# Cross-attention on one core: the value products of a unit in two halves of 8 tiles

## The reference

```python
q = _split_heads(hidden_states @ w_q, HEADS)
k = _split_heads(text @ w_k, HEADS)
v = _split_heads(text @ w_v, HEADS)
out_text = _merge_heads(_sdpa(q, k, v))
k_ip = _split_heads(ip_h @ w_k_ip, HEADS)
v_ip = _split_heads(ip_h @ w_v_ip, HEADS)
out_ip = _merge_heads(_sdpa(q, k_ip, v_ip, mask=mask_ip))   # mask from boxes on a 64 x 32 grid
out = (out_text + IP_SCALE * out_ip) @ w_out + b_out + residual
```

## Time and profile before

| | us |
|---|---|
| median of 3 runs | 456.08 (455.82 to 456.23) |
| profiled execution, its own time | 456.7 |
| its span, first to last instruction | 454.9 |
| TensorE busy | 431.4 |
| VectorE busy | 351.6 |
| ScalarE, GpSimd busy | 133.1, 157.0 |

### The profile page before, as it was taken

How to read it: one execution, slowest core, us unless ns; L and a number is a source line. 1 busy time by engine, 2 the same in 40 slices (tenths; PEclk the granted TensorE clock), 3 DMA queues, 4 the chain that set the end, 5 groups by cost and what they waited for, 6 DMA issues and landing times.

```text
span 454.9 us, 14459 instructions
## 1 busy us (share of the span) xinstructions
PE 431.4 (95%) x6594; PEld 336.6 (74%) x6594; DVE 351.6 (77%) x466; ACT 133.1 (29%) x190; POOL 157.0 (35%) x129
## 2 busy tenths in 40 slices
PE   2877999989999999999999999999999999999997
PEld 2856678867777777777777777777777777777775
DVE  0722578989888888889978898888888988888712
ACT  2402265535222432232233322243223322222200
POOL 1500255845522542336222652254233622232200
PEclk9969799999999999999999999999999999999999
DMA  8998022230213311142113221331124211112333
GB/s 315 340 399 316 1 62 87 71 96 3 63 55 122 115 48 49 48 159 93 54 49 117 96 71 55 128 101 49 48 66 158 82 49 48 49 49 71 101 135 115
DMA packets 23726, 46.97 MB, mean 103 GB/s; under 512 B 2673, under 2 KB 2801, under 8 KB 23665
## 3 DMA queue, kind: packets, MB, share of 16 engines
q1 hardware_dynamic: 23664, 46.05, 29.8%
HBM read 35.55 MB, written 10.49 MB: 101 GB/s over the span
## 4 chain that ended last, share of the span: by engine, by line
PE 92%; DVE 3%; DMA 2%; issue 1%; SPq 1%; ACT 1%
PE ps L557 65%; PE ps L598 12%; PE ps L582 10%; PE ps L641 2%; DMA eye_sb<-in_eye 2%; PE ps L631 1%; PE ps L670 1%; DVE x_lo L507 1%; DVE prob_t L489 1%; DVE prob_t L490 1%; SPq L233 1%; PE ps L646 0%; DVE prob_t L487 0%; DVE text_max L420 0%; DVE prob L426 0%
## 5 line engine op out<-in xcount | busy, mean ns | idle before, releaser
L307 POOL TENSOR_TENSOR prob<-prob,rden 128x1104 f32<-128x1104 f32 x40 | 82.4, 2059 | 262.2 <-DVE rden L449 262.2
L557 PE MATMUL ps<-x_hi,wq_hi 128*128 128x512 f32 x200 | 84.6, 423 | 4.0 <-DVE x_lo L507 4.0
L339 ACT ACTIVATE q<-ps 128x512 f32<-128x512 f32 x40 | 23.8, 595 | 213.2 <-PE ps L557 213.2
L557 PE MATMUL ps<-o_hi,wo_hi 128*128 128x512 f32 x200 | 82.7, 414 | 0.0
L557 PE MATMUL ps<-x_hi,wq_lo 128*128 128x512 f32 x200 | 80.7, 404 | 0.0
L557 PE MATMUL ps<-x_lo,wq_hi 128*128 128x512 f32 x200 | 79.9, 400 | 0.0
L557 PE MATMUL ps<-o_lo,wo_hi 128*128 128x512 f32 x200 | 79.1, 395 | 0.0
L557 PE MATMUL ps<-o_hi,wo_lo 128*128 128x512 f32 x200 | 79.0, 395 | 0.0
L420 DVE TENSOR_REDUCE text_max<-ps 128x16 f32<-128x1104 f32 x40 | 51.9, 1298 | 27.2 <-PE ps L582 27.2
L444 DVE TENSOR_REDUCE den<-prob 128x16 f32<-128x1104 f32 x40 | 52.0, 1301 | 24.4 <-ACT prob L343 24.4
L456 DVE STREAM_TRANSPOSE prob_t<-prob 128x1536 f32<-128x1536 f32 x40 | 70.7, 1769 | 0.1
(11 more groups left out here) (47 smaller groups left out, 382.2 us busy)
## 6 DMA issues: line engine op xcount, KB each, us to landing
stage<-in_x SPq DMA_DIRECT2D x43, 256.0 KB, 3.3
res<-in_x SPq DMA_DIRECT2D x37, 256.0 KB, 2.7
out_tiles<-res SPq DMA_DIRECT2D x37, 256.0 KB, 2.0
wk_raw<-in_w_k SPq DMA_DIRECT2D x2, 1280.0 KB, 8.7
wki_raw<-in_w_k_ip SPq DMA_DIRECT2D x2, 1280.0 KB, 7.7
wv_raw<-in_w_v SPq DMA_DIRECT2D x2, 1280.0 KB, 14.3
wvi_raw<-in_w_v_ip SPq DMA_DIRECT2D x2, 1280.0 KB, 17.9
stage<-in_w_q SPq DMA_DIRECT2D x5, 320.0 KB, 8.1
```

The source lines that it names most:

```text
L307: nc.gpsimd.tensor_tensor(e[:, :, 0:TEXT], e[:, :, 0:TEXT], rden[:, par, 0, :].unsqueeze(2).to_broadcast([P, QT * HG, TEXT]), ALU.mult)
L339: nc.scalar.activation(q[:, c % 2, :], ps[:, Q_BANK, :], ACT.Copy, scale=SCALE).then_inc(q_copied, 1)
L557: last = nc.tensor.matmul(ps[:, bank, :], w[:, kt, cols], m[:, b, kt, :], start=(n == 0), stop=(n == len(steps) - 1))
```

## The change

The loops of make_o are put in another order. Before, token block kb is the outer loop, and inside it all four row groups a and four heads j: 16 products on 16 tiles, then the same 16 tiles for the next token block. After, the row groups are taken in pairs: for row groups 0 and 1 all three token blocks (24 products on 8 tiles, each tile used every 8 products), then the same for row groups 2 and 3. The products themselves, their operands, start and stop, the waits ahead and the signal on the last one are the same.

```diff
-                for kb in range(KB):
-                    for a in range(QB):
-                        rows = slice(SQ * a, SQ * a + SQ)
-                        p_t = prob_t[rows, c % 2, :, SQ * kb:SQ * kb + SQ].rearrange("p (n h) r -> p n h r", h=HG)
-                        for j in range(HG):
-                            last = nc.tensor.matmul(ps[DH * j:DH * j + DH, a, O_COL:O_COL + QT * SQ],
-                                                    v[rows, KB * b + kb, P * g + DH * j:P * g + DH * j + DH], p_t[:, :, j, :],
-                                                    start=(kb == 0), stop=(kb == KB - 1))
+                for kb, a in [(kb, a) for pair in ((0, 1), (2, 3)) for kb in range(KB) for a in pair]:
+                    rows = slice(SQ * a, SQ * a + SQ)
+                    p_t = prob_t[rows, c % 2, :, SQ * kb:SQ * kb + SQ].rearrange("p (n h) r -> p n h r", h=HG)
+                    for j in range(HG):
+                        last = nc.tensor.matmul(ps[DH * j:DH * j + DH, a, O_COL:O_COL + QT * SQ],
+                                                v[rows, KB * b + kb, P * g + DH * j:P * g + DH * j + DH], p_t[:, :, j, :],
+                                                start=(kb == 0), stop=(kb == KB - 1))
                 last.then_inc(o_made, 1)
```

## The result

The changed kernel took 459.67 us (458.79 to 460.19, 4 runs) against 456.15 us for the kernel before (455.82 to 456.62, 4 runs): ratio 1.0074, 95% interval 1.0056 to 1.0093, slower by 3.5 us. The profiled execution took 459.46 us, its span 457.7, 2.8 more than the span before. One execution of the changed kernel in the first experiment, the profiled one, took 2300.48 us, with units of 52.7 us from start to end; it is left out everywhere, and nothing is read from its trace.

A forecast was written before the change was run, and what follows sets the result against it. The prediction took TensorE's own work as the bound, every other engine having slack. The last pass moves from 1.215 to 1.320, 0.105 us per burst, times 40 is 4.2; 456.08 + 4.2 = 460.3 us, range 458.8 to 464.0.

The forecast's parts named there:

- The bound: TensorE's own work bounds the kernel; any time value products gain or lose counts for the whole kernel, 40 times.
- The rules: Value-product burst: first 64 instructions 0.0067 us a product, later 0.0167, 64 outstanding, 0.109 between passes on one tile, 0.025 load to pass.
- The two terms that the trace of before did not show: In the new burst: 0.109 us between successive products on one tile; product 25's second pass holds product 26 until 0.650.
- The sum for the bursts: Last pass at 1.320 instead of 1.215, so 0.105 us more per burst; 40 bursts give 4.2 us.
- what stands behind a burst: The 0.20 us after the last pass stays; o_hi copy, o_lo subtraction and the next unit only shift, costed at nothing.
- unit 9.92 us long, other groups unchanged: Sign in the changed profile: a unit of 9.92 us in place of 9.82, with the other groups of work unchanged.
- the dearer one: Next weights not loaded under a tile's running pass; each return costs 0.136, +0.186 per burst, 7.4 us, 463.5; chance 0.14.
- The faster one: Stalls occur only with all 16 tiles having work outstanding; with 8 the stream flows, 0.26 less per burst, 445.7 us; chance 0.10.
- The one without a hold: No change: places not held in order, product 25 doesn't hold product 26; last pass 1.236, +0.7 us, 456.8; chance 0.08.
- tile time: Time a tile is occupied in a burst: passes of 128 columns follow 0.109 us apart on one tile.
- places and flow: Places: 64 instructions outstanding, freed in program order as work ends; flow: 0.0167 us a product after the first 64 instructions.

The follow-up runs named there:

- the first experiment: The changed kernel measured again, against the kernel before in more rounds: 459.69 us against 455.37, ratio 1.0075.
- the quarters: Kernel before's loops reordered to one row group, or one head, at a time, each tile used again after 4 products: 478.57 us (ratio 1.0496) and 475.89 us (1.0448).
- turning back: Kernel before with token block 1 on row groups 2, 3, 0, 1; some returns after 8 products, without halves: 455.68 against 455.37 us, ratio 1.0009.
- two blocks: Kernel before's order with the third token block left out, 32 products per burst: 441.38 us, ratio 0.9678.
- two blocks in halves: The change's order with the third token block left out, row groups 0 and 1 first, then 2 and 3: 443.40 us, ratio 0.9741.
- early second half: The change's halves A and B interleaved as A0 A1 B0 A2 B1 B2, so the second starts before the first ends: 458.41 us, ratio 1.0062.
- halves less 4: The change's order without its last 4 products (token block 2 of row group 3): 456.88 us against 455.76 for the kernel before, ratio 1.0017.
- less 8: The change's order without its last 8 products (token block 2 of row groups 2 and 3), 40 left: one run of 454.39 us.
- full plus 4: Kernel before's order with 4 products more, token block 2 again on row group 0: one run of 466.70 us.
- quarters by head: Kernel before's loops reordered to one head at a time with all four row groups, tiles used again after 4 products: 475.89 us, ratio 1.0448.
- halves by head: The change with halves by head instead of row group: heads 0 and 1 on all row groups, then 2 and 3: 459.34 us, ratio 1.0072.
- 8 more: Kernel before's order with 8 products more, token block 2 again on row groups 0 and 1: 468.69 us, ratio 1.0279.

## Why the prediction was right

The forecast was 460.3 us, +4.2; measured were 459.67, +3.5, and in the repeat +3.4 by the ratio. Step by step:

The bound was right: TensorE waits for nothing in the steady part before or after, and a longer burst lengthens every unit.

The rules, read mainly from one burst of the kernel before, were right for every order that was tried but the quarters. Last passes, forecast and read: before 1.215 and 1.218, change 1.320 and 1.322, turning back 1.215 and 1.218, two blocks 0.799 and 0.800, two blocks in halves 0.884 and 0.885, early second half 1.300 and 1.302, halves less 4 and less 8 1.254 and 1.255, 1.102 and 1.104, full plus 4 1.431 and 1.433. The two terms that the trace of before did not show came out as taken: 0.109 from product to product on one tile (passes of products 1, 9 and 17 at 0.024, 0.242 and 0.461, two passes apart each), and product 26 held behind product 25 to 0.65. The sum for the bursts, 4.2 us, was measured as 4.20.

The term that was mis-sized is what stands behind a burst, which I costed at nothing. The 0.20 us to the next work stayed (0.198), but the 15 out passes became 0.017 shorter and the 15 q passes 0.021, 0.038 per unit and 1.15 us in all. So the sign "unit 9.92 us long, other groups unchanged" did not come out: the steady unit is 9.89. With this term the forecast would have been 459.1, and the span's difference is 2.8.

Of the rivals, the dearer one (0.136 at each return) would have had the last pass at 1.40; it was at 1.32, and halves and quarters by head fell together with those by row group. The rule of the Trainium skill that it leaned on ("TensorE: Matmul & The Clock Gate", what overlaps and what doesn't) is not borne out by these rows. The faster one fell with the two blocks in halves (product 17 at 0.318 with only 8 tiles used before it). The one without a hold needed product 26 at 0.566 and product 26 was loaded at 0.65; its price was also a little off, since 1.236 - 1.215 is 0.021 a burst, 0.8 us and not 0.7.

What stays open: why the projections run faster behind the change. Over the experiments the q passes took 3.625 us in every order whose last passes were set by tile time (the change, halves by head, both quarters, early second half, halves less 4 and less 8) and 3.645 to 3.650 where they were set by places and flow (before, turning back, two blocks in either order, full sweeps with 4 and 8 more). That is a relation and not a cause, and the out passes (3.681 to 3.698) follow it only in part. The same profiles show that it isn't the length of the unit. The trace shows where the time lies: in a steady unit the q passes stand 0.224 to 0.236 us apart at first and 0.227 later, and the later spacing begins with pass 7 in the change and with passes 10 to 12 before; of the out passes it is mainly the last that is shorter, 0.318 to the next work in place of 0.328.

## What to carry to other kernels

When small products run on many tiles of the array at once, count instructions in flight, not tiles: read in the trace at which product the stream first stops, and compare the moment when it goes on with the end of the work that stands that many instructions back. And before a total is set against a sum, look at the clock row of its profile: here a fall in one unit was worth 1.4 to 3.0 us, nearly as much as the change itself. An order of products is good if the stream, with its stalls, takes at least as long to come back to a tile as the tile is busy with its last product, here 0.218 us (two passes of 0.109). With 16 tiles at a time the stalls covered that. With 8 at a time the stream is back after 8 products, in 0.05 us at the start and 0.13 later (8 x 0.0067 and 8 x 0.0167), and it stands until the tile is free. A return to a tile after few products is free where the stream is being held up anyway.

## What the runs showed of the hardware

A float32 product on a 32x32 tile is two loads and two passes, and its passes of 128 columns stood 0.109 us apart on one tile, whether within a product or from one to the next. The first 64 instructions of a burst come at 0.0067 us per product, the others at 0.0167. The stalls that tile time does not explain fit a bound of 64 instructions outstanding, with a place free 0.027 us after the end of the instruction 64 back, in program order (the ends are those that the profile models). With tile time this gave the last pass to 0.004 us in eleven kernels, one of them the kernel that it was read from. New to me was the limit inside the 64: a product on an unused tile, 13th in the quarters, was not issued past the waiting products before it until 0.27, in both kinds of quarters; their bursts were 0.07 longer than by the bound of 64 alone. And TensorE's granted clock fell from 2.4 to 1.2 GHz in the fifth unit of seven of thirteen profiles, behind waits of 0.9 and 1.5 us that all thirteen have.
